# Second layer of a two-layer model: activation ring, held-back second products, decays in batches

## The reference

```
u  = xn                                            # 2048 x 128
dt = softplus(u @ W_dt.T + b_dt)                   # per token and feature
for n in range(16):                                # 16 states for each feature
    s_n[t] = exp(-exp(A_log[:, n]) * dt[t]) * s_n[t-1] + dt[t] * u[t]
y  = sum_n (B[:, n] * C[:, n]) * s_n + D * u
p  = softmax(xn @ router_w + router_b)             # 64 experts, the top 8 kept, rescaled to sum 1
routed = sum_e cw[:, e] * (silu(xn @ W1[e] + B1[e]) @ W2[e] + B2[e])     # hidden size 32
shared = sum over 2 experts of silu(xn @ SW1 + SB1) @ SW2 + SB2          # hidden size 256
out = x + y + routed + shared
```

## Time and profile before

| what | value |
|---|---|
| time, median of 3 runs | 469.74 us (465.57 to 470.54) |
| span of the profiled execution | 473.9 us (the page gives no other time for it) |
| PE busy | 346.5 us, 73% |
| DVE busy | 347.8 us, 73% |
| ACT busy | 261.5 us, 55% |
| POOL busy | 243.2 us, 51% |
| first multiply of an expert unit | starts at 322.51 us |
| first of the last sums on DVE | starts at 464.05 us |

### The profile page before, as it was taken

The page is one execution under the profiler, slowest core; times in us unless marked ns, Lnnn a source line. Parts: engine busy times, 40 slices in busy tenths (PEclk is TensorE's granted clock), DMA queues, the critical chain, the costliest instruction groups (busy, mean ns, idle before and its releaser), DMA issues.

```text
span 473.9 us, 5780 instructions
## 1 busy us (share of the span) xinstructions
PE 346.5 (73%) x1491; PEld 247.2 (52%) x1491; DVE 347.8 (73%) x615; ACT 261.5 (55%) x440; POOL 243.2 (51%) x254
## 2 busy tenths in 40 slices
PE   1846879667975987779506848977887887887883
PEld 0435659356854866668403524544554554554542
DVE  5679998897864866648169759908688688688674
ACT  1477654546458346374505675355856856856820
POOL 3475300704763676776800049005577877877850
PEclk9977675959997898998956975997999999999997
DMA  6374100100111112120160000004658658668574
GB/s 175 94 200 128 25 1 1 45 11 24 46 39 29 34 41 81 43 42 21 35 190 0 0 0 2 0 0 89 126 101 161 123 116 163 122 119 162 112 152 111
DMA packets 36213, 35.09 MB, mean 74 GB/s; under 512 B 12166, under 2 KB 30839, under 8 KB 36183
## 3 DMA queue, kind: packets, MB, share of 16 engines
q0 software_dynamic: 7104, 21.90, 22.7%
q1 hardware_dynamic: 29078, 12.84, 10.2%
HBM read 13.29 MB, written 4.65 MB: 38 GB/s over the span
## 4 chain that ended last, share of the span: by engine, by line
PE 35%; POOL 19%; DVE 19%; issue 13%; ACT 6%; DMA 3%; another core or an unknown queue 2%; DVEq 1%; SPq 0%; POOLq 0%; ACTq 0%
POOL state L568 10%; PE psum L1376 5%; POOL xn_tok L572 4%; PE psum L1349 4%; POOL g_hi L581 3%; PE psum L1365 3%; PE psum L1389 3%; PE psum L1443 3%; PE psum L292 3%; PE psum L293 2%; PE psum L294 2%; PE psum L1352 2%; PE psum L1355 2%; PE psum L1338 1%
## 5 line engine op out<-in xcount | busy, mean ns | idle before, releaser
L1212 DVE TENSOR_TENSOR_SCAN state<-dec,win_t 128x1024 f32<-128x1024 f32 x32 | 73.4, 2293 | 26.5 <-ACT dec L777 26.5
L568 POOL TENSOR_SCALAR state<-state,ssm_cb 128x1024 f32<-128x1024 f32 x32 | 49.7, 1553 | 48.0 <-DVE state L1212 45.0
L812 ACT ACTIVATE sil<-psum,vec_t 128x512 f32<-128x512 f32 x64 | 43.2, 687 | 48.3 <-PE psum L294 37.7
L509 POOL DMA_INDIRECT parts<-t_out,part x39 | 41.0, 1050 | 48.3 <-ACT t_out L726 41.9
L1498 PE MATMUL psum<-hid,g_w 128*128 128x512 f32 x128 | 62.1, 599 | 0.0
L1221 DVE TENSOR_TENSOR hid<-sil,psum 128x512 f32<-128x512 f32 x64 | 41.7, 676 | 12.9 <-ACT sil L812 10.9
L497 POOL DMA_INDIRECT x_tile<-normed,token x39 | 41.3, 1059 | 13.4 <-issue 10.7
L292 PE MATMUL psum<-xn_hi,g_hi 128*128 128x512 f32 x64 | 39.7, 620 | 11.3 <-ACT sil L812 11.3
L1094 DVE TENSOR_TENSOR t_hid<-t_sil,psum 128x352 f32<-128x352 f32 x39 | 20.3, 521 | 32.3 <-ACT t_sil L710 23.5
L717 ACT ACTIVATE t_hid_t<-psum 128x384 f32<-128x384 f32 x39 | 19.2, 492 | 38.9 <-PE psum L1365 25.3
L1376 PE MATMUL psum<-w_out,t_hid_t 128*128 x234 | 37.5, 300 | 2.2 <-ACT t_out L726 1.4
(11 more groups left out here) (308 smaller groups left out, 887.6 us busy)
## 6 DMA issues: line engine op xcount, KB each, us to landing
xn_tok<-state POOLq DMA_DIRECT2D x32, 512.0 KB, 4.5
e_raw<-in_L_ffn_w SPq DMA_DIRECT2D x16, 128.0 KB, 2.2
both<-parts SPq DMA_DIRECT2D x4, 512.0 KB, 5.6
e_raw<-in_L_ffn_w SPq DMA_DIRECT2D x8, 176.0 KB, 2.6
res<-in_L_attn_x SPq DMA_DIRECT2D x4, 256.0 KB, 3.8
normed<-rows SPq DMA_DIRECT2D x1, 1024.0 KB, 5.2
g_raw<-in_L_ffn_w SPq DMA_DIRECT2D x16, 64.0 KB, 2.3
g_w<-in_L_ffn_w SPq DMA_DIRECT2D x16, 64.0 KB, 2.2
```

The lines of the kernel that those rows point to most:

```text
L509: pool.indirect_dma_start(out=parts, out_offset=bass.IndirectOffsetOnAxis(ap=part[:, n:n + 1], axis=0), in_=t_out[n % ORING][:, :], in_off ...
L568: own(pool.tensor_scalar(state[k][:, :], state[k][:, :], ssm_cb[:, i * GPI + k // 2:i * GPI + k // 2 + 1], 0.0, ALU.mult, ALU.add))
L812: act.activation(sil[:, c % 2, :], ps[c % 2][:, :], ACT.Silu, bias=vec_t[:, V_B1 + c // NBLK:V_B1 + c // NBLK + 1]).then_inc(h_silu, 1)
L1212: dve.tensor_tensor_scan(state[k][:, :], dec[n % DECS][:, at_half], win_t[:, at_half], 0.0, ALU.mult, ALU.add).then_inc(scanned, 1)
```

## The change

It is all in the second layer.

1. **Buffers.** `hid` becomes one ring of eight buffers, for shared and expert units alike; `sil` a ring of four; `dec` six buffers, four of them laid over memory that earlier stages have left.
2. **PE.** One loop over 80 units u (16 shared, then the 64 expert units, u = c + 16). At step u it does the weights matmul of the next unit, the input product of the one after that, and the second products up to unit u − `behind(u)`. `behind` is 2, rises to 3, 4, 5, 6 over the four steps ahead of the last one before a batch, and is 1 in that last one, where so six second products come together.
3. **ACT.** The decays come in six batches, of 2, 3, 3, 3, 3 and 2, ahead of the silus of u = 14, 23, 35, 47, 58 and 67 (`DECAYS_AT`).
4. **DVE.** A list (`SCAN_BEFORE`) says ahead of which multiply each of the 32 scans comes: in expert units 0, 0, 2, 4, then 10, 11, 13, 15, 17, 18, then 22, 23, 25, 27, 29, 30, then 34, 35, 37, 39, 41, 42, then 45, 46, 48, 50, 52, 53, then 54, 55, 57, 59.
5. **POOL.** Scaling and DMA of a state are two functions; the split of a group's weights goes ahead of the state of a scan that the list ties to it. D·u is written behind the scaling of state 0.
6. **Softplus.** ACT does bias add, Abs and Exp of each block in turn, then two Squares (half of the polynomial of blocks 2 and 3), then four Ln with a bias just under 1. The polynomial is completed by DVE in two instructions, and a maximum takes the place of mask and copy.
7. **Order ahead of the loop.** Two time-step products come ahead of the logits' transposes; the router's exponential comes ahead of shared silu 6 instead of 4; the gate weights are turned at step 11 instead of 4; DVE does the softplus of block 2 ahead of the gate weights and all others ahead of their split.

The diff, cut to its core:

```
+        HRING, SRING, DECS = 8, 4, 6
...
+        WEIGHTS_AT, CW_AT, COPIES_AT = 6, 11, 12
+        DECAYS_AT = {14: (0, 1), 23: (2, 3, 4), 35: (5, 6, 7), 47: (8, 9, 10), 58: (11, 12, 13), 67: (14, 15)}
+        SCAN_BEFORE = [SHARED, SHARED, SHARED + 2, SHARED + 4]
+        for u0 in (23, 35, 47, 58):
+            SCAN_BEFORE += [u0 + 3, u0 + 4, u0 + 6, u0 + 8, u0 + 10, u0 + 11]
+        SCAN_BEFORE = [u - SHARED for u in SCAN_BEFORE + [70, 71, 73, 75]]
...
+        def behind(u):
+            for at_unit in (WEIGHTS_AT, *DECAYS_AT):
+                if 0 <= at_unit - 1 - u <= 4:
+                    return (1, 6, 5, 4, 3)[at_unit - 1 - u]
+            return 2
...
             # POOL
+            pool.wait_ge(var_ready, 3)
+            for j in range(4):
+                clear_firsts(j)
+            pool.nop().then_inc(firsts_ready, 1)
...
+            pool.wait_ge(win_ready, NBLK)
+            for j in range(4, DECS):
+                clear_firsts(j)
+            pool.nop().then_inc(firsts_ready, 1)
...
+            weigh_state(0)
             pool.wait_ge(cw_turned, NBLK)
             own(pool.tensor_scalar(y_t, u_t, vec_t[:, V_D:V_D + 1], 0.0, ALU.mult, ALU.add))
+            add_state(0)
+            g = GPI
+            for k in range(1, NSCAN):
+                while g < NG and (g - GPI + 1) * NBLK <= SCAN_BEFORE[k]:
+                    split_next(g)
+                    g += 1
+                weigh_state(k)
+                add_state(k)
...
             # ACT
+                e = softplus_bufs[b][0]
+                own(act.activation(e[:, :], blk(dt_t, b), ACT.Abs))
+                own(act.activation(e[:, :], e[:, :], ACT.Exp, scale=-1.0))
+                act.nop().then_inc(sp_exp, 1)
+            for b in range(POOL_LOGS, NBLK):
+                e, _, p = softplus_bufs[b]
+                act.activation(p[:, :], e[:, :], ACT.Square, scale=0.5, bias=half_mid[:, 0:1])
+            for b in range(NBLK):
+                e, l, _ = softplus_bufs[b]
+                act.activation(l[:, :], e[:, :], ACT.Ln, bias=under_one[:, 0:1]).then_inc(sp_log, 1)
...
+            for u in range(SHARED + UNITS):
+                if u == WEIGHTS_AT:
                     act.wait_ge(r1_arg, 1)
                     act.activation(pair[:, :, :], pair[:, :, :], ACT.Exp).then_inc(r1_exp, 1)
+                if u == min(DECAYS_AT):
+                    act.wait_ge(win_ready, NBLK)
+                for n in DECAYS_AT.get(u, ()):
+                    decay(n)
+                if u == COPIES_AT:
                     for b in range(NBLK):
                         copy_cw(b)
+                if u < SHARED:
+                    shared_silu(u)
+                else:
+                    silu(u - SHARED)
...
             # DVE
+            def softplus(b):
+                e, l, p = softplus_bufs[b]
+                dve.wait_ge(sp_log, b + 1)
+                if b < POOL_LOGS:
+                    dve.wait_ge(sp_poly, b + 1)
+                    own(dve.tensor_tensor(l[:, :], l[:, :], p[:, :], ALU.max))
+                else:
+                    own(dve.scalar_tensor_tensor(e[:, :], e[:, :], ROOT, e[:, :], ALU.subtract, ALU.mult))
+                    own(dve.scalar_tensor_tensor(p[:, :], p[:, :], LEFT / 4, e[:, :], ALU.add, ALU.mult))
+                    own(dve.scalar_tensor_tensor(l[:, :], p[:, :], -1.0, l[:, :], ALU.mult, ALU.max))
+                own(dve.scalar_tensor_tensor(blk(dt_t, b), blk(dt_t, b), 0.0, l[:, :], ALU.max, ALU.add))
+                own(dve.tensor_tensor(blk(win_t, b), blk(dt_t, b), blk(u_t, b), ALU.mult))
...
+            softplus(3)
+            softplus(0)
+            softplus(1)
+            for b in range(NBLK):
+                split_cw(b)
+            dve.wait_ge(firsts_ready, 1)
+            k = 0
+            for c in range(UNITS):
+                while k < NSCAN and SCAN_BEFORE[k] == c:
+                    scan(k)
+                    k += 1
+                weigh(c)
...
             # PE
+            for u in range(SHARED + UNITS):
+                if u == CW_AT:
                     turn_cw(0)
                     turn_cw(1)
                     second_biases(0)
                     turn_cw(2)
                     second_biases(1)
                     turn_cw(3)
                     second_biases(2)
                     second_biases(3)
+                if SHARED <= u + 1 < SHARED + UNITS:
+                    expert_weights(u + 1 - SHARED)
+                if u + 2 < SHARED:
+                    shared_in(u + 2)
+                elif u + 2 < SHARED + UNITS:
+                    expert_in(u + 2 - SHARED)
+                while done <= u - behind(u):
+                    if done < SHARED:
+                        shared_out(done)
+                    else:
+                        expert_out(done - SHARED)
+                    done += 1
```

More of the change, by code:

```diff
@@ L561, in _, with split_next @@
+            def split_next(g):
+                j = g % GPI
+                pool.wait_ge(g_in[j], (g // GPI) * 16 + 16)
+                pool.wait_ge(cwx_made, (g - GPI + 1) * NBLK)
+                split_group(g, j)
+            weigh_state(0)
             pool.wait_ge(cw_turned, NBLK)
             own(pool.tensor_scalar(y_t, u_t, vec_t[:, V_D:V_D + 1], 0.0, ALU.mult, ALU.add))
-            def group_turn(i, last):
-                for k in range(SCANS):
-                    pool.wait_ge(scanned, i * SCANS + k + 1)
-                    own(pool.tensor_scalar(state[k][:, :], state[k][:, :], ssm_cb[:, i * GPI + k // 2:i * GPI + k // 2 + 1],
-                                           0.0, ALU.mult, ALU.add))
-                    if i > 0 or k >= 2:
-                        pool.wait_ge(y_in[(k + 2) % SCANS], 16 * (i + k // 2))
-                    pool.dma_start(y_t[:, (k % 2) * HALF:(k % 2 + 1) * HALF], state[k][:, :], accum_op=ALU.add
-                                   ).then_inc(y_in[k], 16)
-                    if k % 2 == 1 and not last:
-                        split_next(i, k // 2)
@@ L779, in decay, with silu @@
                                scale=ssm_a[:, n:n + 1]).then_inc(decay_ready, 1)
-            for c in range(NSH * NBLK):
-                k, tb = divmod(c, NBLK)
-                if c in range(NBLK):
-                    own(act.activation(softplus_bufs[c][0][:, :], blk(dt_t, c), ACT.Abs))
-                if c == AHEAD_OF_CW:
+            def silu(c):
+                act.wait_ge(h_made, c + 1)
+                if c >= SRING:
+                    act.wait_ge(hid_done, c - SRING + 1)
+                act.activation(sil[c % SRING][:, :], ps[c % 2][:, :], ACT.Silu,
+                               bias=vec_t[:, V_B1 + c // NBLK:V_B1 + c // NBLK + 1]).then_inc(h_silu, 1)
```

256 lines of the change are left out of this document (109 added, 147 removed).

## The result

The changed kernel takes 482.66 us (median of 4 runs, 479.93 to 484.86), the kernel before 468.58 (4 runs, 465.57 to 470.54): a ratio of 1.031, 95% interval 1.024 to 1.037. The forecast was 466.1, and its range ended at 475.

A forecast was written before the change was run, and what follows sets the result against it. No engine was full; PE and DVE had floors near 14 us in a 17.7 us turn. Preparation −5.4, D·u +1.2 and loop +0.6 made −3.6 us, a median of 466.1 us; range 455 to 475.

The forecast's parts named there:

- The preparation: Ahead of the expert loop: first expert multiply at 317.1 instead of 322.51, −5.4 us, between −8.3 and 0.
- the walk: Instruction-by-instruction timing of the new schedule, from the time-step work to the last sum; its loop came to 142.1 us.
- 0 (PE at half speed throughout): Slow bound of the preparation's gain: nothing gained if PE runs at half speed all through it.
- y = D·u: POOL's D·u right behind the first scaled state: DVE's third scan meets it, +1.2 us, between 0 and 2.2.
- the stretch to the fifth scan: Start of the new expert loop, from the first multiply to the fifth scan: 18.2 us.
- The period: Twelve units, six scans and one batch of three decays: 28.5 us, against 26.6 for the old loop.
- Eleven units: Piece whose batch, ahead of unit 42, stands next to no group border: 23.5 us.
- The last piece: From the scan ahead of unit 45 to DVE's last sum: 43.4 us, POOL trailing by one, last DMA landing 4.6 late.
- POOL keeps up: Rival: group 5's split ready near 6.5 and scans earlier; 4 to 10 us beyond the forecast, 460 us, chance 0.26.
- time 0: Start of the walked period, the scan ahead of unit 15; there the state loses to the scan by hundredths.
- The clock falls in the batch: Rival: half-speed PE at product 20 and held products, two periods, 3.5 us each; +3.4, 473.1 us, chance 0.34.

The follow-up runs named there:

- the first experiment: New preparation and buffers of the changed kernel with the old expert loop: 466.81 us, 0.998 of the kernel before.
- With the exponential first: Changed kernel with the router's exponential ahead of all shared silus instead of ahead of the seventh: 476.08 us, 1.019 of the kernel before.
- without splits: Changed kernel without POOL's splits of groups 2 to 15, so its output isn't the layer's: 461.49 us, 0.984 of the kernel before.
- raw order and early split: Changed kernel with raw first weights fetched ahead of second weights on SP and POOL's split up to two units earlier: 473.88 us, 1.011 of the kernel before.
- the four fillers: Changed kernel with eleven extra weights matmuls ahead of each of the input products 20, 32, 52 and 60: 479.68 us, 1.025 of the kernel before.
- 469.88: Changed kernel with evenly spread scans, no second products held back in expert units and the router's exponential first: 469.88 us, 1.008 of the kernel before.
- 471.68: Changed loop with even scans, nothing held back in expert units, exponential first, early split and SP's raw weights first: 471.68 us, 1.009 of the kernel before.
- the old loop with the exponential first: New preparation with the old expert loop, and the router's exponential ahead of all shared silus: 459.25 us, 0.984 of the kernel before.

## Why the prediction was wrong, step by step

**The preparation (−5.4, measured −0.6): mis-sized.** With the 7.6 us added to the times of the changed kernel's profile, its stations are late against the walk, and more so from one to the next. ACT's first bias add is at 263.0 where the walk had 261.8, the first shared silu at 278.4 instead of 276.3. DVE uses the exponential at 280.14 + 7.6 = 287.8 instead of 285.4; the softplus is done 2.2 us late; the last silu ahead of the decays ends 3.7 us behind even the slow end of its 306.7 to 309.0; the first multiply is at 321.9, not 317.1. So half of the 4.8 us was lost by the end of the softplus, half behind it. The softplus instructions were priced well (at 0.72 to 0.73, as taken). What was mis-sized is the chain of PE and ACT, above all its last part, from the split of the gate weights to the last silu. The granted clock is 1.00 from 254 to 264 and from 277.5 to 293, and half speed in these three stretches:

```profile
250.00:254.00 4.00, 3.95 (x10) 2.24 (x11) 3.19 (x5) 1.47 (x3) 0.00 (x0) 0.54 0.00 0
271.00:277.00 6.00, 5.47 (x13) 4.18 (x14) 2.39 (x4) 3.11 (x5) 0.00 (x0) 0.50 0.00 0
296.00:308.00 12.00, 12.00 (x22) 6.05 (x22) 1.39 (x2) 6.29 (x8) 0.00 (x0) 0.50 0.00 0
```

The first belongs to this execution: in the first experiment, with the same preparation, the clock from 250 to 254 is 1.00 and the bias add comes 9.2 us behind the reciprocal, near the forecast's 9.4, instead of 10.6; yet the first multiply is still 68.7 behind it, which makes the gain 1.3. The last is the dear one: PE idles 3.96 us until DVE has split the gate weights, and then works 12 us without a pause at 1.2 GHz, and the last silu ahead of the decays waits for it. With the exponential first PE has no such wait, the clock is 1.00 from 290 to 306, and the first multiply comes 8.1 us earlier. So I take this half speed as a consequence of the late exponential. That −0.6 lies next to the bound "0 (PE at half speed throughout)" is luck: PE was not at half speed throughout.

**y = D·u (+1.2) and the stretch to the fifth scan (18.2).** Together 19.4, measured 335.51 − 314.30 = 21.2, and 19.6 without splits: the missing 1.6 I put down to one more late split, ahead of unit 8 (PE waits 1.40 us for it at 325.56), which the walk did not visit.

**The period (28.5 twice; measured 30.0 and 30.9).** Mechanism right, size off by 3.9 in all. The walk's stations stand in the trace: the decays hold ACT, the state loses its race against the scan, the split ends at 9.7, the product goes at 9.8. Two terms were short. The burst of held products ran at 0.57 of the clock, so multiply 21 ends at 365.53, that is at 19.9 instead of 18.3: 1.6 us, as much as the burst is longer than at full clock. And scans do wait for a POOL instruction in flight: 2.52 and 3.06 us at 365.53 and 368.55, against 2.28, together 1.0 where the forecast had 0.65.

**Eleven units (23.5; measured 24.3).** Right within 0.8: this batch stands next to no group border, and no product waits for a split here.

**The last piece (43.4; measured 53.3): the step that failed.** 9.9 of the 16.3 us that the loop missed are here. The walk took it that "POOL trails by one" and that only DMA landing counts. In the trace three group borders, 52, 56 and 60, lie in this piece, and PE waits at each:

```profile
433.76 0.50 PE L298 MATMUL psum<-xn_hi,g_hi 128*128 128x512 f32 x1 [2.42 <-POOLq L569]
...
447.75 0.50 PE L298 MATMUL psum<-xn_hi,g_hi 128*128 128x512 f32 x1 [1.45 <-POOLq L569]
...
461.02 0.79 PE L298 MATMUL psum<-xn_hi,g_hi 128*128 128x512 f32 x1 [3.34 <-POOLq L569]
```

The middle one is not POOL's own order: its split began at 443.40 after 4.86 us of waiting for raw weights. Without splits the piece is 450.94 − 407.23 = 43.7 us, the forecast to 0.3. So the walk was right for a POOL without splits, and it had not applied its own period's finding, that a product at a group border waits for a split behind two states, at the borders here.

**Measured against forecast, piece by piece:** (first multiply to fifth scan, two periods, eleven units, last piece)

| piece | forecast | after | no splits | raw order and early split |
|---|---|---|---|---|
| to the fifth scan | 19.4 | 21.2 | 19.6 | 19.6 |
| period 1 | 28.5 | 30.0 | 26.4 | 30.2 |
| period 2 | 28.5 | 30.9 | 26.4 | 28.8 |
| eleven units | 23.5 | 24.3 | 24.0 | 24.2 |
| last piece | 43.4 | 53.3 | 43.7 | 49.4 |
| sum | 143.3 | 159.6 | 140.2 | 152.1 |

**A queue I had left out.** The prediction charged held-back products to PE alone. They also keep second-weight buffers, SP waits for those, and raw weights queue behind it. The run with SP's raw weights in front shows what this cost: 4.7 us of loop, and no wait for raw weights left. It was there to be read in the code: a wait, and what is queued behind it.

**The rivals.** "POOL keeps up" needed the state to win its race at time 0; it lost it at 345.73 by 0.10 us. Without splits a period is 26.4, against the 25.7 given for a POOL in time. "The clock falls in the batch" happened, at both places named, at a price of 1.6 us for the first (6.91 against 5.31 at full clock) where 3.5 was taken; the four fillers together brought 3 us. Right in mechanism and sign, it carried the smaller part of the loss. What the prediction held against it was misread: in the earlier trace rows the digit for 319.9 to 331.7, the first slice of the old loop, is a 7, and the granted clock from 324 to 328 is 0.50 there, behind 6.22 us of idle PE.

**What the six batches could have brought.** Even without any split the new loop takes 140.2 us, the old one 140.6 (with or without splits). So the two pairs of table loads saved brought nothing that the loop's length shows. What this change won was in the preparation, and it came out only once the exponential went first.

**Not settled:** why the new loop at its best with the splits in it (469.88 and 471.68) is over 10 us behind the old one; the loops are 153.1 and 155.3 against 140.6. The trace shows 24.2 us of idle PE at five batches, with the granted clock at 0.50 behind the one looked at (353 to 358), while in the old loop with the exponential first it is 1.00 from 308 to 440; that this is all of it was not shown. A ring deeper than two groups, which would let the split go early with products held back, was not tried.

## What to carry to other kernels

Work that is held back keeps its buffers, so follow every hold to the queue that waits for the buffer, and to what stands behind that wait in the same queue; here it was the next group's input. Where two waits stand in series on one resource, mending one alone may only move the wait (15.9 to 9.3 us at one place, 9.7 to 26.6 at the other, and 0.1 us of loop): look at which wait grew before calling a cause refuted. And a period's finding belongs in every other piece of the walk that has the same border.

## What the runs showed of the hardware

A scan waits for a POOL instruction that is already running, by a little less than the overlap. At 368.34 a scaled state of 1.13 us begins, the scan behind it at 368.55 takes 3.06:

```profile
368.34 1.13 POOL L602 TENSOR_SCALAR state<-state,ssm_cb 128x1024 f32<-128x1024 f32 x1 [0.21 <-POOL sel_now L568]
```

The state ends at 369.47, 0.92 into the scan, which is 0.78 longer than the usual 2.28. The prediction had this for a tensor_scalar alone. The Trainium skill, SBUF — State Buffer, Two separate sides, says that such instructions exclude each other and that the one that started keeps the ports; the trace agrees, for the scan too. Even a CAST of 128x128, 0.29 us when alone, takes 2.17 at 365.96, beside a scan.

A table load is 1.28 us at every place in the profiles of the two kernels, and the decays begin 0.02 us behind its end:

```profile
350.49 1.28 ACT L840 ACT_TABLE_LOAD   x1
351.79 5.78 ACT L840 ACTIVATE dec<-dt_t,ssm_a 128x2044 f32<-128x2044 f32 x3
```

The Trainium skill, ScalarE: Activation LUTs, What ACT_TABLE_LOAD costs, gives about 1.28 us for the load, with which the trace agrees, and about 1.38 us more for a drain, together about 2.66 us for a switch. With the drain the trace disagrees: a batch with both loads, 350.49 to 358.88, is 8.39 us against 8.4 forecast from the rows, and the measurement decides.
